# A graph-network kernel on one core: sorting stage on 128 lanes with stacked base pieces, and four small stages moved into its block

## The reference

```python
x = _layernorm(x + _L0_gnn_ref(x, edge_index, edge_attr_16, edge_type_7, ...))        # graph attention, two layers
x = _layernorm(x + _L1_gnn_ref(x, edge_attr_12, edge_weight, edge_index, ...))        # convolution with radial filters
x = _layernorm(x + _L2_gnn_ref(x, L2_gnn_weight, ..., edge_type_8, 6250))             # relational layer
x = _layernorm(x + _L3_gnn_ref(x, edge_index, edge_weight, L3_gnn_W, ...))            # gated sums over the source
```

```python
row, col = (edge_index[0], edge_index[1])        # row = src, col = dst
msg = gated[col] * edge_values[:, None]
out = jax.ops.segment_sum(msg, row, num_segments=n)
```

## Time and profile before

| | |
|---|---|
| median of three runs | 7712.72 us |
| time of the profiled execution | 7716.48 us |
| its span in the profile | 7714.7 us |
| granted TensorE clock, mean over the span | 0.77 |
| PE, DVE, ACT, POOL busy | 71%, 59%, 25%, 62% |
| start of `phase_order` (first DVE instruction) | 133.63 us |
| first rank matmul | 164.41 us |
| end of the ranks (last copy under mask) | 316.74 us |
| start of `phase_terms_rows` (first MEMSET) | 387.12 us |

### The profile page before, as it was taken

One profiled execution on the slowest core, in us unless ns is written; L12 is line 12 of the kernel. 1 busy time (PEld: TensorE's weight loads), 2 busy tenths in 40 slices (PEclk: granted clock), 3 DMA queues, 4 the chain that ended last, 5 costly groups with the idle time before them and its releaser, 6 DMA issues. The chain is left out here.

```text
span 7714.7 us, 103020 instructions
## 1 busy us (share of the span) xinstructions
PE 5501.5 (71%) x21382; PEld 3803.1 (49%) x21383; DVE 4562.5 (59%) x9626; ACT 1960.2 (25%) x6454; POOL 4805.4 (62%) x4886
## 2 busy tenths in 40 slices
PE   5768999977699999675677778995565554565550
PEld 2235565544566555454666664443444443444440
DVE  5357777777577777767344443223444456666667
ACT  0036666632366666332000001110000001000002
POOL 0017777765477777655777776777777733777750
PEclk8578999986889999866555557997777777777775
DMA  0075455522345545223111112433333323333322
GB/s 17 25 164 143 136 135 135 136 73 63 122 133 135 135 134 137 59 66 91 31 31 31 31 31 76 125 118 103 105 105 105 105 87 117 106 105 105 105 76 69
DMA packets 431408, 733.88 MB, mean 95 GB/s; under 512 B 112552, under 2 KB 278777, under 8 KB 429718
## 3 DMA queue, kind: packets, MB, share of 16 engines
q0 software_dynamic: 212352, 484.47, 24.0%
q1 hardware_dynamic: 217510, 246.12, 10.5%
q10 hardware_dynamic: 1348, 1.21, 0.0%
HBM read 610.03 MB, written 121.40 MB: 95 GB/s over the span
## 5 line engine op out<-in xcount | busy, mean ns | idle before, releaser
L746 POOL DMA_INDIRECT at_x<-table,at_idx x1664 | 1575.6, 947 | 587.8 <-issue 525.6
L821 PE MATMUL at_psO<-at_x,at_main 128*128 128x273 f32 x3328 | 1032.2, 434 | 157.3 <-DVE agg L1011 156.7
L1242 POOL DMA_INDIRECT order<-pay,pos x784 | 823.1, 1050 | 391.1 <-issue 245.0
L2789 PE MATMUL so_psO<-source_ring,so_hot 128*128 x1664 | 603.8, 540 | 489.2 <-issue 381.4
L2771 POOL DMA_INDIRECT source_ring<-gated_rows,so_idx x784 | 749.0, 955 | 286.5 <-issue 232.7
L2023 POOL DMA_INDIRECT conv_x<-conv_table,conv_idx x784 | 755.7, 964 | 263.7 <-issue 238.7
L2198 PE MATMUL rel_psO<-rel_ring,rel_hot 128*128 x1664 | 596.6, 536 | 449.4 <-issue 257.6
L2179 POOL DMA_INDIRECT rel_ring<-rel_table,rel_idx x784 | 741.3, 946 | 250.5 <-issue 237.9
L821 PEld LDWEIGHTS at_psO<-at_x,at_main 128*128 128x128 f32 x3328 | 606.3, 200 | 529.7 <-issue 412.1
L1011 DVE TENSOR_TENSOR agg<-agg,at_psO 128x273 f32 x1664 | 725.7, 436 | 221.6 <-DVE agg L1011 169.3
L2789 PEld LDWEIGHTS so_psO<-source_ring,so_hot 128*128 128x128 f32 x1664 | 458.9, 283 | 634.0 <-issue 531.4
(11 more groups left out here) (487 smaller groups left out, 8292.5 us busy)
## 6 DMA issues: line engine op xcount, KB each, us to landing
at_place<-places SPq DMA_DIRECT2D x208, 256.0 KB, 3.7
rel_table<-cr_rows SPq DMA_DIRECT2D x50, 1024.0 KB
at_x<-table,at_idx POOLq DMA_INDIRECT x1664
pj_x<-table SPq DMA_DIRECT2D x20, 640.0 KB, 4.2
order<-pay,pos POOLq DMA_INDIRECT x784, 2.1
conv_x<-conv_table,conv_idx POOLq DMA_INDIRECT x784, 2.4
rel_ring<-rel_table,rel_idx POOLq DMA_INDIRECT x784, 2.7
source_ring<-gated_rows,so_idx POOLq DMA_INDIRECT x784, 2.8
```

The costliest lines, as they stand in the source:

```text
L746: pool.indirect_dma_start(x[b][:, j, 0:TABW], None, d.table[0:NR, :], bass.IndirectOffsetOnAxis(ap=idx[b][:, j:j + 1], axis=0)).then_inc(x ...
L821: ins = nc.tensor.matmul(psO[j % BANKS][:, 0:AGG], main[b % 2][:, j, :], x[b][:, j, 0:AGG], start=True, stop=True)
L1242: pool.indirect_dma_start(d.order[0:TP * P, :], bass.IndirectOffsetOnAxis(ap=m.pos[:, t:t + 1], axis=0), m.pay[:, t, :], None).then_inc(pl ...
L2789: ins = nc.tensor.matmul(psO[j][:, 0:K], hot[b][:, j, :], x[:, bass.ds(ts[j] * K, K)], start=True, stop=True)
```

## The change

**One.** The sorting works on 128 lanes of 784 edges (`TP`) instead of 112 rows of 896. For that `phase_index` turns a fifth table (row 6, the bucket numbers) into `m.qsrc`. All operations of `phase_order` on a whole array go over 784 elements, and `pos` needs no turning at the end.

**Two.** The two base pieces stand stacked in one tile `pieces` of 115 partitions: 64 (of which 51 hold the high piece), then 51 with the low one. One matmul against `pick` of 115 partitions adds both, so a bucket takes four matmuls instead of six. The counting gives its sums on 115 partitions, so that both copies of the base come out of one scan.

**Three.** The slot rows are computed on 104 partitions of 8 words instead of one of 832.

**Four.** `phase_places`, `phase_edge_weights`, `phase_conv_weights` and `phase_table_weights` for layer 1 are gone as blocks. Their work is in the block of `phase_order`: the turning first on the tensor engine, the convolution weights' matmuls after the counting, the six copies after the scan on the vector engine, the weights' arithmetic at its end, all loads first in the sync engine's stream, and the 18 stores before the slot rows' stores.

The core of the diff:

```diff
-    TILE_ROWS = (1, 2, 3, 0)
+    TILE_ROWS = (1, 2, 3, 0, 6)
...
-        rows = sb("rows", [TCP, 6, TCH, P])
+        rows = sb("rows", [TCP, 7, TCH, P])
...
-                for k, to in enumerate((src_tile[:], rel_tile[:], w_tile[:], m.pay[:, :, 0])):
+                for k, to in enumerate((src_tile[:], rel_tile[:], w_tile[:], m.pay[:, :, 0], m.qsrc[:])):
...
-        hot = sb("hot", [TCP, NB, L], F16)
+        hot = sb("hot", [P, NB, TP], F16)
-        one = sb("one", [NB, NB, TCP], F16)
-        many = sb("many", [NB, NB, TCP], F16)
+        pick = sb("pick", [NU, NB, P], F16)
...
+                v.memset(wt[:], 0.0).then_inc(zeroed, 1)
+                ch.do(v.tensor_scalar(col[:, 0:UP], m.iota[:, 0:UP], float(NB - 1), None, ALU.is_equal))
+                ch.link(v.tensor_scalar(col[:, UP:NB - 1 + NU], m.iota[:, 0:NB - 1 + NU - UP], float(NB - 1), None, ALU.is_equal))
...
+                dve.wait_ge(turned, 1)
+                v.tensor_copy(places[:, 0:4, :], psR[0][:, 0, :].rearrange("p (c e) -> p c e", e=P))
...
-                ch.link(v.tensor_copy(whole, cum[:]))
-                ch.link(v.tensor_copy(hi[:], whole))
-                v.scalar_tensor_tensor(out=lo[:], in0=hi[:], scalar=-64.0, in1=cnt[:], op0=ALU.mult, op1=ALU.add).then_inc(pieces_ready, 1)
+                ch.link(v.tensor_copy(whole[:], cum[:]))
+                ch.do(v.tensor_copy(pieces[0:UP, :], whole[0:UP, :]))
+                ch.link(v.tensor_copy(high[UP:NU, :], whole[UP:NU, :]))
+                v.scalar_tensor_tensor(out=pieces[UP:NU, :], in0=high[UP:NU, :], scalar=-64.0, in1=cnt[UP:NU, :], op0=ALU.mult, op1=ALU.add).then_inc(pieces_ready, 1)
...
             def _(pe):
+                for c in range(SCH):
+                    n = P if c < FULL else REST
+                    nc.tensor.matmul(psR[0][0:n, c // 4, c % 4 * P:(c % 4 + 1) * P], m.loc[:, c * P:c * P + n], m.ident[:], start=True, stop=True)
+                    ins = nc.tensor.matmul(psR[1][0:n, c // 4, c % 4 * P:(c % 4 + 1) * P], m.first[:, c * P:c * P + n], m.ident[:], start=True, stop=True)
+                ins.then_inc(turned, 1)
...
+                pe.wait_ge(copied, 1)
                 for h in range(NB):
                     if h >= 2:
                         pe.wait_ge(picked, h - 1)
                     for e in range(2):
-                        es = slice(e * HL, (e + 1) * HL)
-                        to = psR[h % 2][0:TCP, e, 0:HL]
-                        nc.tensor.matmul(to, before[:], hot[:, h, es], start=True, stop=False)
-                        nc.tensor.matmul(to, one[:, h, :], lo[:, es], start=False, stop=False)
-                        ins = nc.tensor.matmul(to, many[:, h, :], hi[:, es], start=False, stop=True)
+                        nc.tensor.matmul(psR[h % 2][:, e, 0:HL], before[:], hot[:, h, e * HL:(e + 1) * HL], start=True, stop=False)
+                    for e in range(2):
+                        ins = nc.tensor.matmul(psR[h % 2][:, e, 0:HL], pick[:, h, :], pieces[:, e * HL:(e + 1) * HL], start=False, stop=True)
                     ins.then_inc(rank_ready, 1)
...
-            phase_order(nc, m, d, phase("order"))
-        phase_places(nc, m, d, phase("pl"))
-        phase_edge_weights(nc, m, d, w, phase("ew"))
-        phase_conv_weights(nc, m, w, phase("cw"))
-        phase_table_weights(nc, m, w, 1, phase("tw1"))
+            phase_order(nc, m, d, w, phase("order"))
```

More of the change, by code:

```diff
@@ L382, in _ @@
                 act.wait_ge(pay_ready, 1)
[L385 to L429, removed]
 def phase_terms_rows(nc, m, d, sem):
@@ L1088, in phase_order @@
[L1088 to L1094 removed]
+        hot = sb("hot", [P, NB, TP], F16)
+        before = sb("before", [P, P], F16)
+        lower = sb("lower", [NB, NU])
+        col = sb("col", [P, NB - 1 + NU], F16)
+        pick = sb("pick", [NU, NB, P], F16)
+        inner = sb("inner", [NB, 2], F16)
@@ L1095, in phase_order @@
+        none = sb("none", [NU, TP])
+        cnt = sb("cnt", [NU, TP])
+        cum = sb("cum", [NU, TP])
+        whole = sb("whole", [NU, TP], I32)
+        high = sb("high", [NU, TP], F16)
+        pieces = sb("pieces", [NU, TP], F16)
+        base = sb("base", [NU, 4])
         base_i = sb("base_i", [NB, 1], I32)
         reached = sb("reached", [NB, S], F16)
[L1097 to L1100, removed]
@@ new lines, in phase_order @@
+        tring = sb("tring", [NG, GROUP], I32)
+        pad_rows = sb("pad_rows", [1, 2, 2 * GROUP], I32)
+        places = sb("places", [P, SCH, P], BF16)
+        flags = sb("flags", [P, SCH, P])
+        wt = sb("wt", [39, 2, D])
+        ae = sb("ae", [39, 2, D])
+        self_pick = sb("self_pick", [39, P])
+        pk = sb("pk", [39, 3])
+        wn = sb("wn", [FILT, D])
+        l1T = sb("l1T", [FILT, FILT])
+        l2 = sb("l2", [FILT, FILT])
+        b2 = sb("b2", [FILT, 1])
+        wmT = sb("wmT", [FILT, D])
@@ new lines, in _ @@
+                wch.wait()
+                for k in range(2):
+                    wch.do(v.tensor_reduce(m.w_table[:, k, D:D + 2 * H], prod[:, k, :, :].rearrange("p a (h c) -> p (a h) c", c=C), AX_X, ALU.add))
+                dve.wait_ge(conv_ready, 1)
+                dve.wait_ge(self_ready, 1)
+                wch.do(v.tensor_copy(m.w_conv_in[:], psI))
+                wch.do(v.tensor_copy(m.w_conv_out[:], psW[:, 0, :]))
+                wch.do(v.tensor_copy(m.b_conv_out[:], psW[0:1, 1, :]))
@@ L1221, in _ @@
-                pe.wait_ge(place_ready, 1)
-                for c in range(TCH):
-                    ins = nc.tensor.matmul(psR[0][0:P, c // 4, c % 4 * TCP:(c % 4 + 1) * TCP], pos[:, c * P:(c + 1) * P], m.ident[0:TCP, 0:TCP], start=True, stop=True)
-                ins.then_inc(turned, 1)
+                        nc.tensor.matmul(psR[h % 2][:, e, 0:HL], before[:], hot[:, h, e * HL:(e + 1) * HL], start=True, stop=False)
+                    for e in range(2):
+                        ins = nc.tensor.matmul(psR[h % 2][:, e, 0:HL], pick[:, h, :], pieces[:, e * HL:(e + 1) * HL], start=False, stop=True)
@@ L1226, in _ @@
+                    ins.then_inc(rank_ready, 1)
+                pe.wait_ge(at_ready, 1)
+                for j in range(GROUP):
+                    ins = nc.tensor.matmul(psN[:, j:j + 1], reached[:, j:S:GROUP], inner[:, 0:1], start=True, stop=True)
+                ins.then_inc(slots_ready, 1)
+                pe.wait_ge(folded, 1)
+                nc.tensor.matmul(psSelf, self_pick[:], m.fold[:, 0:2 * H], start=True, stop=True).then_inc(self_ready, 1)
             @block.scalar
             def _(act):
-                nc.scalar.copy(one[:], m.ident[0:NB, 0:NB].unsqueeze(2).to_broadcast([NB, NB, TCP]))
```

247 lines of the change are left out of this document (116 added, 131 removed).

## The result

| | before | after |
|---|---|---|
| median, first comparison (4 runs each) | 7711.57 us (7707.02 to 7715.18) | 7580.69 us (7579.05 to 7581.71) |
| median, second comparison (9 and 5 runs) | 7718.63 us (7712.61 to 7721.03) | 7583.50 us (7579.73 to 7588.89) |
| time of the profiled execution | 7716.48 us | 7579.05 us |
| its span | 7714.7 us | 7577.4 us |

The ratio is 0.983 with a 95% interval of 0.9813 to 0.9847, and 0.9825 (0.9812 to 0.9838) in the second comparison. The change makes the kernel 131 to 135 us faster. The forecast was 7571 us, the range 7560 to 7590: the time lies in the range, 10 us above the forecast and above the forecast's own, narrower range (7563 to 7577).

What follows compares the result with a forecast made beforehand. No engine bounds the whole program; the edited stretch gains in full. Terms sum to -142.1 us: profiled 7716.5 becomes 7574.4, its median 7570.6, say 7571 us. Own range 7563 to 7577, with low clock and one bare-load case 7560 to 7590.

Steps and rivals of the forecast that it cites:

- start of the block: A fifth turned table in `phase_index` delays the sorting block by 1.6 us.
- counting: DVE's first instruction to counted sums, now with 28 tiles turned first: 22.5 us becomes 23.1, +0.6 us.
- bases: Counted sums to first rank matmul, 8.3 us before: +2.1 us, from the six copies and one more conversion, less narrower operations.
- ranks: The 51 buckets' matmuls and copies: clock rises, DVE sets the pace at 1.07 us a bucket, 57.9 against 152.3 us, -94.4.
- recoding and slot rows: After the ranks: 784 instead of 896 columns and twelve short chained steps, 19.1 us becomes 10.4, -8.7.
- four stages: The small stages before `phase_terms_rows` move beside the sort: 51.3 us becomes 8.0 (bounds 7.5 to 12), -43.3.
- MEMSET: First one of `phase_terms_rows`, behind all edited work: starts at 245.0 instead of 387.1 us, -142.1.
- rival with the low clock: In the ranks the clock never rises: 1.36 instead of 1.07 us a bucket, 7585 us; chance 0.17 for never or partly up.
- Bare loads: In the ranks every load lies unhidden at 0.17 us: 1.33 us a bucket, 7584 us, or 7617 with low clock; chance 0.06.
- The loop that it gave at 0.99 us a bucket: Two-buffer loop in the ranks at high clock: PE's matmuls, handover and copy take 1.98 us for two buckets, so DVE sets pace.
- late end of the block: Loads or stores late at the sorting block's end return up to 10 of the small stages' 43 us: 7581; chance 0.05.
- slow case: Ranks: copy of 2.5 us beside PE's writes, low clock, bare loads: 4.8 us a bucket, 7759; no gain or slower, 0.02.

Runs made afterwards that it cites:

- e1: The kernel before, with the pieces and their pickers zero-padded from 51 to 112 partitions, still six matmuls a bucket: 7628.23 us, ranks 71.7 us.
- e2: The changed kernel without the stacking: low piece in its own tile, three matmuls of 128, 51 and 51 rows per half: 7642.02 us.
- e4: The kernel before, with 150 extra matmuls of 51 rows and then 150 of 112 rows put ahead of the ranks: 7795.58 us.
- e7: The changed kernel with PE allowed one bucket ahead instead of two, so PE and DVE alternate: 7649.69 us.
- e9: The changed kernel with PE only one bucket ahead, plus 60 full-row matmuls ahead of the ranks: 7657.71 us.
- e5: The changed kernel with the ranks' copies going in turn into two tiles, added at the end: 7577.31 us, after beside it 7583.50.
- e3: The changed kernel with the four small stages again as blocks of their own behind the sorting: 7609.72 us.
- e11: The changed kernel run once more, unaltered: median 7583.50 us.
- e10: The kernel before, with the tile of index rows 7 rows wide instead of 6, the seventh unused: 7711.27 us.

## Why the prediction was right

By its own terms, in us:

| term | predicted | measured |
|---|---|---|
| start of the block | +1.6 | +4.0 (133.63 to 137.65) |
| counting | +0.6 | -0.1 (22.5 to 22.4) |
| bases | +2.1 | +2.0 (8.3 to 10.2) |
| ranks | -94.4 | -92.2 |
| recoding and slot rows | -8.7 | -8.8 |
| four stages | -43.3 | -44.0 |
| MEMSET | -142.1 | -139.1 |

**The clock.** The step on which two thirds hung held: full rows, 1.00 from some 6 us into the ranks on. The rival with the low clock does not fit (1.13 us a bucket, not 1.36). e1, e2 and e4 show the reason as the prediction had it, the 51 rows; of the two features that it named (short rows, bare loads) the first alone is enough to keep the clock low; whether bare loads alone would was not tried. What it left open, e7 and e9 answer: a pause of 0.29 us a bucket is borne, one of about 1 us isn't. Its argument for staying up (66% busy in `phase_terms_rows`) was thin: that the clock stayed up was in part luck, since with PE one bucket ahead in place of two (e7) it is 0.50 throughout the ranks.

**Bare loads.** Starts 0.17 us apart at 128 and 115 rows: the loads are hidden, as the counting had suggested, and against the sentence of the Trainium skill that the prediction cites (TensorE: Matmul & The Clock Gate, Part 3, The mechanism). The same section also lets a load go ahead into a background weight buffer, which these rows can't show. e1 has hidden loads at six matmuls of one height.

**The mis-sized terms.** A chained copy was put 0.04 us behind the end of the one before, by a row of counting; it was 0.10, so 1.13 and not 1.07 us a bucket. For 51 that is 3.1 us, of which 0.9 was given back by other terms of the ranks. The loop that it gave at 0.99 us a bucket was right: e5, where it binds, has 0.98. The start of the block was taken as one more table, 1.6; the table took 1.4 (3.89 us of delay at `pay` less 2.49 at the slot rows). The rest was not in the sum: 1.84 from the first loads, 0.65 between them and the slot rows, 0.1 behind. For the 0.65, the matmuls of line 351 start 0.69 us apart for the first 5.7 us in after and for the first 4.3 us in before, and 0.35 apart from then on; the windows view of 57.3 to 60.0 us has 5 of them in after and 10 in before. The distance halves as it does when the clock rises from 0.50 to 1.00, but the view has no low clock there, so that this is argued and not shown.

**The rest of the distance.** 7580.7 us against 7570.6: 3.0 from the terms, 1.7 behind the memset, and 5.4 because the profiled execution of before stood 3.8 above the median used, and that of after 1.6 below its own. The forecast's own range (7563 to 7577) allowed 2.5 us for this last, too little: the median of before alone was 7711.6 in one comparison and 7718.6 in the other. The time lies in the wide range because that was stretched for a low clock and bare loads, neither of which came. It is also, to the us, the 7581 that the prediction gave for a late end of the block. So the total alone doesn't tell the forecast from its rivals; the rows do.

**Slips in the working.** The terms given for the forecast's own range, counting +-3, block end +4 and 2.5 between runs, add up to 7565 to 7580, not 7563 to 7577. With the pace of 1.99 + 0.3 us beside the copy, the kernel would be slower than before from a copy of 1.6 us on, not 2.2. The 28 turned tiles are 14 matmuls with two records each; they took 5.4 us in after, and the clock rose 4.7 us into them, which is why counting came out 0.7 us under its term. None of this moves the forecast.

**The other rivals.** The late end of the block did not come (7.2 us for the rest, DVE's work and 1.3 us of the block's end). A copy did not slow down beside PE's writes (1.03 us as taken), so the slow case had nothing to stand on. e3 shows the four stages' term as it stood: +44.2 us in the stages, less 4.5 in counting and bases and 0.8 in the block's start.

## What to carry to other kernels

Where a matmul stage shows a clock of 0.50 while PE is busy all the time, look at the partitions of its operands before counting its instructions: padding with zeros gave 80 us here for two memsets and wider pickers. Give PE a second buffer before judging the clock, since a PE that waits for each result loses it. When the consumer then sets the pace, look at what its instruction waits for: an accumulation in place that waits for its own last write costs more than its duration, and two targets in turn take that away, until the loop of the two buffers sets the pace.

## What was not expected

- Operations of DVE that don't wait for each other overlap a little: copies of 1.03 us started 0.98 us apart in the mean (e5). The rows of before had shown it: the one-hots, 0.40 us long, start 0.30 us apart.
- A clock that had risen was lost with PE never idle, when two of three matmuls filled 51 rows (e4, 251.6 to 255.7 us at 1.00, then 0.50).
- What lies behind the memset, with the same instructions in every kernel, took from 7320.1 us (e1) to 7335.7 (e11) over the thirteen profiled executions. The five in which the small stages were blocks of their own (before, e1, e3, e4, e10) average 7323, the other eight 7331, in small amounts over many phases. Whether a part of the gain is given back there, or this is chance, isn't settled; it is at most some 8 us of 139.
